# A four-layer model on one core: the first feed-forward part's lookup summed on TensorE, layer 2's token lookup on four column tiles, shared expert weights requested in the norms, and zero matmuls in every norm

## The reference

```
x = x + 0.5 * ffn(layernorm(x));  x = x + attn(layernorm(x));  x = x + 0.5 * ffn(layernorm(x))
```

```
gx  = xp[buf_tok]                                  # gather rows by expert
gu  = einsum('ech,ehi->eci', gx, gate_up_proj);  hid = silu(g) * u
eo  = einsum('eci,eih->ech', hid, down_proj) * buf_w[..., None]
out = zeros(...).at[buf_tok].add(eo)               # add back to the tokens
```

## Time and profile before

| what | value |
|---|---|
| median of three executions | 2566.09 us (2560.04 to 2567.62) |
| the profiled execution | 2557.84 us, span 2556.1 us |
| TensorE's mean granted clock in it | 0.861 of full |
| busy share: PE, DVE, ACT, POOL | 75%, 55%, 34%, 23% |
| the first layer 0 FFN | 16.0 to 203.2 us |
| the layer 1 FFNs | 469.9 to 600.2 us, 822.8 to 952.2 us |
| the layer 2 FFNs | 961.6 to 1142.6 us, 2088.7 to 2272.6 us |
| a norm | 9.4 us, twelve times |

### The profile page before, as it was taken

How to read it: one execution, slowest core, us unless ns; L and a number is a source line. 1 busy time by engine, 2 the same in 40 slices (tenths; PEclk the granted TensorE clock), 3 DMA queues, 4 the chain that set the end, 5 groups by cost and what they waited for, 6 DMA issues and landing times. The chain is left out here.

```text
span 2556.1 us, 39583 instructions
## 1 busy us (share of the span) xinstructions
PE 1906.4 (75%) x14831; PEld 1377.5 (54%) x14831; DVE 1405.2 (55%) x3242; ACT 861.5 (34%) x1917; POOL 599.9 (23%) x614
## 2 busy tenths in 40 slices
PE   1265578796998867626999989998998686728458
PEld 1123454465777445424767766776677664515355
DVE  7976642333563346544676777667767227343541
ACT  0002321221552212224665566556665211201110
POOL 5752220231000323632111121112111005620200
PEclk7677889896998987767999999999999887758669
...
GB/s 145 0 0 13 1 5 0 110 167 40 198 1 21 154 61 185 236 132 51 19 18 18 19 35 18 18 18 35 18 18 2 34 96 188 162 177 3 9 4 19
DMA packets 56617, 156.56 MB, mean 61 GB/s; under 512 B 12803, under 2 KB 32157, under 8 KB 52158
## 3 DMA queue, kind: packets, MB, share of 16 engines
...
...
## 5 line engine op out<-in xcount | busy, mean ns | idle before, releaser
L2041 PE MATMUL l_heads_ps_p<-xnT,l_heads_w 128*128 128x512 f32 x512 | 249.4, 612 | 27.7 <-ACT l_heads_taps L2232 19.5
L2386 DVE SCALAR_TENSOR_TENSOR l_heads_taps<-l_heads_padded,l_heads_conv,l_heads_taps 128x1024 f32<-128x1024 f32 x144 | 191.8, 1333 | 10.4 <-ACT l_heads_taps L2232 9.2
L2059 PE MATMUL l_heads_bank<-l_heads_mz,l_heads_mt 64*64 64x128 f32 (+1 forms) x2560 | 161.2, 266 | 2.1 <-DVE l_heads_mz L2423 2.1
L2570 POOL TENSOR_SCALAR l_heads_rstd<-l_heads_mean_var 128x8 f32<-128x8 f32 x16 | 3.9, 246 | 651.2 <-DVE l_heads_mean_var L2452 651.2
L2059 PEld LDWEIGHTS l_heads_bank<-l_heads_mz,l_heads_mt 64*64 64x64 f32 x2560 | 129.8, 135 | 42.6 <-issue 38.2
L2041 PEld LDWEIGHTS l_heads_ps_p<-xnT,l_heads_w 128*128 128x128 f32 x512 | 88.3, 191 | 99.9 <-issue 62.8
L2418 DVE COPY l_heads_mz<-l_heads_bank 128x256 f32<-128x256 f32 x160 | 67.1, 420 | 112.5 <-PE l_heads_bank L2065 112.3
L296 PE MATMUL l_ffn_a_ps_gate<-xnT,l_w 128*115 128x512 f32 x48 | 31.8, 799 | 109.7 <-DVE l_ffn_a_hidden L385 76.7
L205 PE MATMUL norm_turn<-ident,norm_xn 128*128 128x128 f32 x128 | 28.9, 419 | 104.4 <-DVE norm_xn L186 104.4
L282 POOL TENSOR_TENSOR l_ffn_a_other_sum<-l_ffn_a_other_sum,l_ffn_a_other_term 128x716 f32<-128x716 f32 x42 | 93.0, 2215 | 40.3 <-DVE l_ffn_a_other_term L343 40.3
L2065 PE MATMUL l_heads_bank<-l_heads_mt,l_heads_mz 64*64 64x64 f32 x2560 | 101.5, 218 | 0.6 <-ACT l_heads_crossed L2272 0.6
...
## 6 DMA issues: line engine op xcount, KB each, us to landing
...
```

The costliest lines, as they stand in the source:

```text
L2041: mm = pe.matmul(ps_p[half][:], w[b][:, which, c, :], core.xnT[:, c, half * HALF:(half + 1) * HALF], start=(c == 0), stop=(c == KC - 1))
L2059: mm = pe.matmul(bank[c][0][half, s, 0:width * BK], mt[c][half, s, :], mz[c][half, s, 0:width].rearrange("p a n -> p (a n)"), start=True, ...
L2386: dve.scalar_tensor_tensor(out=taps[which][:], in0=padded[which][:, :, j:j + SEQ], scalar=conv[p % 2][:, which, j:j + 1], in1=taps[which][ ...
```

## The change

Four parts, in the order of the program.

1. Norms: TensorE multiplies the zeros five times before the first transpose, 128 x 512, ten records (`WARM`).
2. First layer 0 FFN: a stage of its own (`l0_decode_ffn_stage`). The 16 terms of a unit become ten operands, six pairs added by DVE and four single terms, in five slots. TensorE sums the ten by matmuls with the identity into two PSUM banks (512 and 204 columns), ACT copies them to `w`. POOL adds nothing. The operands of unit u+1 stand between the parts of unit u; there is one `gate` buffer and one pair of banks for gate and up.
3. Layer 1 and 2 FFNs: `Held` requests the router and both shared weights in the norm ahead; the shared weights lie partition by partition in HBM. The expert stage's SP no longer requests them.
4. Layer 2 FFN: group 0 as before (`index_first`), but between the parts of the shared expert; for later groups `parts` is stationary (6 columns) and `hot` moves (128 columns), one pair on each of four column tiles of TensorE. The result lies slot by column, so DVE copies it (`by_slot`), TensorE transposes it (`turn_i`), and DVE masks it by halves (`own`) and makes all addresses over 128 partitions in 7 instructions. `one_hot` comes in two pieces from group 2 on. The weights of the return are ready after group 5, ACT builds 18 diagonal matrices from them in group 6, TensorE sums the return of tiles 2, 5 and 7 (6 products each), DVE the other five, two tiles interleaved; ACT and POOL have no part in the return.

```diff
+WARM = 5
@@ norm_stage, TensorE
+            for i in range(WARM):
+                pe.matmul(turn[:, i % KC, (i // KC) % HALVES, :], core.ident[:], core.zeros[:, 0:HALF],
+                          start=True, stop=True)
@@ l0_ffn_stage
-def l0_ffn_stage(nc, core, name, w, source=None, idle=None):
-    OWN = 7
-    OTHER = LUT - OWN
...
-                        pool.tensor_tensor(total[:], before[:], other_term[n % SLOTS][:], ALU.add)\
-                            .then_inc(other_added, 1)
...
+def l0_decode_ffn_stage(nc, core, name, w, lut, in_idx, out_idx, idle=None):
+    OPERANDS = ((0, 1), (2,), (3, 4), (5,), (6, 7), (8,), (9, 10), (11,), (12, 13), (14, 15))
+    PARTS = (range(0, 4), range(4, 7), range(7, 10))
+    SLOTS = 5
...
+            def decode(u, part):
+                for m in PARTS[part]:
+                    n = u * COUNT + m
+                    if m == 0 and u >= 1:
+                        pe.wait_ge(w_ready, 2 * u)
+                    pe.wait_ge(term_ready, n + 1)
+                    for bank, at in zip(ps_w, columns):
+                        mm = pe.matmul(bank[:, 0:at.stop - at.start], core.ident[:], term[n % SLOTS][:, at],
+                                       start=(m == 0), stop=(m == COUNT - 1))
+                    mm.then_inc(term_summed, 1)
...
+            for u in range(UNITS0):
+                more = u + 1 < UNITS0
+                up(u, 0)
+                if more:
+                    decode(u + 1, 0)
+                up(u, 1)
+                if more:
+                    decode(u + 1, 1)
+                down(u, 0)
+                if more:
+                    decode(u + 1, 2)
+                down(u, 1)
...
+                act.wait_ge(term_summed, COUNT * (u + 1))
+                for bank, at in zip(ps_w, columns):
+                    act.copy(w[:, u, at], bank[:, 0:at.stop - at.start]).then_inc(w_ready, 1)
@@ Router becomes Held; called by norm_stage(..., prefetch=held.load)
+        sp.dma_start(self.router[:], t[f"{layer}_router"].rearrange("(c p) n -> p c n", p=P)).then_inc(self.router_loaded, 16)
+        sp.dma_start(self.shared_in[:], t[f"{layer}_shared_in_w"]).then_inc(self.shared_loaded, 16)
+        sp.dma_start(self.shared_out[:], t[f"{layer}_shared_out_w"]).then_inc(self.shared_loaded, 16)
@@ l2_experts_stage, TensorE
+            def index(g):
+                pe.wait_ge(found_ready, count_of(g - 1))
+                pe.wait_ge(hot_ready, hot_count(g, PAIRS - 1))
+                for i in range(TILES):
+                    for q in range(PAIRS):
+                        e = g * EG + 2 * q
+                        mm = pe.matmul(bank_l[ROWS * q:ROWS * q + 6, 0:P], parts[:, i, e:e + 2, :].rearrange("p j i -> p (j i)"),
+                                       hot[g % 2][:, q, i].rearrange("p j s -> p (j s)"),
+                                       start=(i == 0), stop=(i == TILES - 1), tile_position=(0, ROWS * q))
+                mm.then_inc(i_filled, 1)
+            def turn_i(g):
+                pe.wait_ge(i_copied, g)
+                pe.transpose(bank_l[:, P:2 * P], by_slot[:], core.ident[:]).then_inc(i_turned, 1)
...
+            pe.wait_ge(diagonal_ready, len(BY_PE) * TOP2)
+            for n, i in enumerate(BY_PE):
+                pe.wait_ge(back_loaded[i], 16)
+                for k in range(TOP2):
+                    mm = pe.matmul(pe_sums[n][:, 0:D], diagonal[:, n, k, :], back[i % (2 * SETS)][:, k, :],
+                                   start=(k == 0), stop=(k == TOP2 - 1))
@@ l2_experts_stage, DVE locate(g)
+                    dve.tensor_copy(by_slot[:], bank_l[:, 0:P]).then_inc(i_copied, 1)
+                    dve.wait_ge(i_turned, g)
...
+                dve.tensor_tensor(mine[:, pairs], from_index, own[:, pairs], ALU.mult).then_inc(found_ready, 1)
```

491 lines of the change are left out of this document (293 added, 198 removed).

## The result

| | before | changed |
|---|---|---|
| median of four executions | 2566.55 us | 2482.95 us (2474.78 to 2492.42) |
| ratio, 95% interval | | 0.9681 (0.9639 to 0.9722) |
| profiled execution, its span | 2557.84, 2556.1 us | 2487.11, 2485.4 us |
| mean granted clock in it | 0.861 | 0.900 |

The forecast was 2490 us with a range of 2455 to 2525. The changed kernel is 3.2% faster; the difference of the profiled spans, on which the working rested, is 70.7 us for 70 predicted.

A forecast was written before the change was run, and what follows sets the result against it. DVE and POOL bound the first layer 0 FFN, shared-weight waits layer 1, a chain layer 2. Terms -33 - 16 - 18 - 3 = -70 us: 2488 profiled, 2496 median, forecast 2490; eight in ten between 2455 and 2525.

The forecast's parts named there:

- TensorE's 22.5 us per unit: First layer 0 FFN: ten operands 12.1 us plus up and down 10.4; six units 135 us, with PE the bound.
- the price of an operand: First layer 0 FFN: summing one operand on PE takes two calls, four records, 1.21 us.
- the stalls that I had allowed for the last pairs: First layer 0 FFN: 3.5 us of PE waiting for a unit's last two pairs while DVE finishes the hidden product.
- Both waits: Layer 1 FFNs: PE's waits for shared weights, 8.47 and 7.38 us, go; -16 in the sum.
- my lower bound: Layer 1 FFNs: a gain of only 10 us of the 16, the clock being colder as PE starts 8 us earlier.
- -9: Each layer 2 FFN: front -8, loop +2, tail -3 us; -18 for both.
- The front: Layer 2 FFN before the loop: first take moves by 9 us; -8 for each FFN, bounds -3 and -12.
- The tail: Layer 2 FFN, return after the loop: about -5, diagonals cost 2; net -3 us, bounds -7 and +3.
- the added crossing: Layer 2 loop: DVE's copy, PE's turn and two semaphores per group; +0.3 us per group, 2 per FFN.
- the rival of a growing loop: Layer 2 loop: the crossing costs 2 us per group instead of 0.3, +24 us, whole 2514; 16 in 100.
- +9 for the norms themselves: Norms: zeros delay transposes by 0.7 to 2.4 us in five norms entered at half clock; another two between.
- 12 in all: Stages behind the twelve norms: they start at a higher clock and give back 12 us; net with norms -3.

The follow-up runs named there:

- the weights alone: Kernel before with router and shared expert weights of layers 1 and 2 requested in the norms, nothing else changed: 2546.39 us, ratio 0.9926.
- lookup alone: Kernel before with only the new first layer 0 FFN (l0_decode_ffn_stage), no zero matmuls: 2529.22 us, ratio 0.9841.

## Why the prediction was right

**Layer 0: right, and for its reason.** The stage lost 36.2 us for 33. TensorE's 22.5 us per unit were 22.4 (from 41.03 to 63.46), the price of an operand 1.20 us for 1.21 (three from 58.13 to 61.74), DVE was busy 92.9 us for about 90, and the stage ended at 168.5 for 170.6: the stalls that I had allowed for the last pairs did not come. What the working did not have is that two thirds of this gain lie in POOL's absence alone, and one third in TensorE (all additions on DVE: 162.6 us).

**Layer 1: right in mechanism and, alone, in size.** Both waits went. Alone they gave 14.6 of 16 us. In the changed kernel's trace the first FFN kept only 2.9: its products began with 10 us at half clock, and its loop with 13.7 us at 0.50 [the last window above], 82.4 us for 78.7. On the second chip the same stage takes 119.6 us. In sum the two FFNs gave 10.0, my lower bound, which had "the clock is colder". The clock's record bears out the cold (in the first FFN 34.5 us at the lower level, 21.7 with the weights alone), but not my reason for it, that TensorE starts 8 us earlier: that holds for the weights alone as well. Why the clock was low for longer here is open.

**Layer 2: right in sign, too small.** -14.7 and -14.4 for -9. The front gave 7.3 and 10.4 us for 8, with the takes within 1.3 us of the forecast times. But 2.8 and 2.5 of that are the held weights, which I had priced in layer 1 alone; the new order gave 4.5 and 7.9. The tail gave 5.2 for 3, and the diagonals, 5.4 us of ACT in group 6, count in the loop. The term that was off most is the loop in the first FFN: I had it 2 us longer for the added crossing, and it is 2.3 shorter. In the second it is 1.0 longer, and on the second chip 1.0 longer and 0.5 shorter. So the rival of a growing loop fell. That the crossing is hidden because POOL's takes and puts set the pace is not shown: the traces without it have loops 2 to 5 us shorter, no more than two traces of one loop can differ by.

**Norms: the sum right, its parts wrong.** I forecast +9 for the norms themselves; they were 2.7 us shorter. Missing was that the transposes too run at full clock behind the zeros, 2.67 us for 3.47, which makes a norm entered hot 0.8 to 1.0 us shorter (seven of twelve); three entered cold grew, by 1.1 to 1.4 us. The stages behind show far less than 12 in all: 1.7 and 2.0 us less in layer 3, 2.1 more in the second layer 0 FFN. Nor are these the zeros' alone. Layer 3's 56.8 us stand in all nine traces with zeros, but also, for both FFNs, in two of the five without (lookup alone, and the changed kernel without zeros); the second layer 0 FFN has the same 68.0 us in three traces without zeros. So a difference of 2 us in one pair of traces does not tell what the zeros do. Alone the zeros made nothing that can be told, as forecast; taken out of the changed kernel they cost 18 us by the medians, which the forecast had not.

**The base.** By the medians the change brought 83.6 us, by the profiled executions 70.7: that of before lies 8.7 us below its median, that of after 4.2 above its own. The sum fits the second number, as it was made from it. That it fits to 1 us is luck: the stages that I had priced gave 3 us more in layer 0, 6 less in layer 1, 11 more in layer 2 and 1 more in the norms and behind them, and the stages that I had not priced took 9 us back, 5.5 of them in layer 2's heads.

**The clock in the norms, and the drain.** The Trainium skill, "TensorE: Matmul & The Clock Gate", Part 4: PE-mode transpose, says that transposes do not count as TensorE being busy for the clock. The prediction set against it, and the same trace has a plainer case. Between 1108.1 and 1147.6 us TensorE did nothing, then only the 16 transposes of a norm, to 1151.3; the clock was 0.50 as they began and at its upper level from 1151.2:

```profile
1143.00:1149.00 6.00, 1.39 (x7) 1.36 (x8) 5.32 (x23) 1.58 (x2) 0.00 (x0) 0.50 0.02 3
...
1151.20:1152.30 1.10, 0.08 (x1) 0.00 (x0) 0.69 (x1) 0.59 (x1) 0.00 (x0) 0.98 0.00 0
```

Page and measurement differ, and the measurement decides: float32 transposes do raise the clock here.

"TensorEngine Tiling (Array Packing)" of the Trainium skill, Key Properties, says that a change of tiling mode drains TensorE. No run here prices that drain. The two pairs with and without four column tiles are equal within 2 us by the medians, with intervals of 4 us to either side, over 14 such products: drain, copy and turn together, less what the shorter product saves, are worth at most some 0.4 us each in the whole kernel's time.
